# Differential attention with a fp8 feed-forward: the values' lag in branch 2 falls in steps, the first output blocks leave earlier, and TensorE's program ends in one jump

## The chip, the core and the metric

The kernel runs on one core of a Trainium2 chip. The metric is the device time of one execution in microseconds (us), median of several runs. Engines are named as the profile names them: PE is TensorE (PEld its weight loads, PEq its sequencer), DVE is VectorE, ACT is ScalarE, POOL is GpSimd, SP is SyncE, which only issues DMAs here.

## What is computed

The input x has 1024 rows of 256. The output is x plus two terms, both computed from the layer-normalised x. The second term is a gated feed-forward with its operands cast to fp8.

```python
qkv = x @ Wqkv
q1, k1, q2, k2, v = jnp.split(qkv, [C, 2 * C, 3 * C, 4 * C], axis=-1)   # C = 128, 16 heads
A1 = _causal_sdpa(q1, k1, v)
A2 = _causal_sdpa(q2, k2, v)
diff = A1 - lam * A2
rms = jnp.sqrt(jnp.mean(diff * diff, axis=-1, keepdims=True) + EPS)
diff = (1.0 - LAMBDA_INIT) * diff / rms
attn = out @ Wproj            # out: diff with the heads side by side
ffn = _qdot(gelu(_qdot(x, w_gating[0])) * _qdot(x, w_gating[1]), w_linear)
```

`_causal_sdpa` is a causal softmax attention. Each head has queries and keys of 8 and values of 16. So there are two softmaxes (branches 1 and 2) over the same values.

## The kernel before, in words

All matrices of the attention are held transposed: keys on the partitions, queries along the free axis. The 16 heads of a branch are four **groups** of four heads, so both branches make eight groups, g = 0 to 7; groups 4 to 7 are branch 2. The causal score matrix of a head is cut into nine **chunks** of 512 columns (table CHUNKS, c = 0 to 8), some of them in two pieces (kb, wide, q0): the key block, the number of query blocks, the first query. Chunks 0 to 2 finish the queries of the first half (0 to 511); chunk 2 (MIXED) also opens the second half, and chunk 8 (LAST) ends it.

Chunks times four heads are 36 items of a group, taken three at a time: a **unit** n has three score matmuls (`scores`, L898) into one of two PSUM areas, and one exponential of 1536 columns on ACT (L442). A group has 12 units and the whole attention 96 (UNITS). POOL zeroes the upper triangle of the chunks in DIAGONALS (`mask`, L366). Then PE multiplies the exponentials by the values (`values`, L910) into PSUM bank 6, which holds one half of the queries of one group at a time. When a half is done DVE copies it out transposed (`take(g, h)`, L594), and PE may open the next half only after that: `values` of chunk 0 waits on o_taken of the group before, `second_half` on o_taken of the first half.

The order on PE is written out by hand. Unit n issues its scores, then each `values(g, c)` whose `due(g, c)` equals n, then what `beside(n)` finds in tables: the later projections of queries and keys in branch 1, the down-projection of the feed-forward (DOWN_AT) in branch 2. `due` is the unit that ends the chunk plus a **lag** in units (the variable late). PE executes in that order and stops at a wait.

In branch 2 DVE makes, for each half of a group, `difference(i, h)`: divide by the sums, subtract from branch 1's result, square, reduce. `inverse_root` (11 short dependent steps) gives the inverse root mean square of the columns it is called with, `scale_by_root` multiplies by it, and `turn_back(p, h)` transposes two groups' result for the output projection and increments out_t_ready: first (0, 0) and (0, 1) for groups 4 and 5, then (1, 0) and (1, 1) for 6 and 7. PE projects with `project(b, p)` (L941) for each block b of 128 rows and both p; `residual` (L947) adds x plus feed-forward by a product with the identity. POOL has added the feed-forward to x before (`residual`, L372), between its masks. The last half's root comes from ACT (L447). SP and ACT send the rows of out, and SP waits until all five DMAs have landed.

Which of the softmax forms is used (with or without exact row maxima) depends on two flags which PE, DVE and SP load and branch on. With this data both flags are 0 and the plain form runs. PE's program holds the other forms behind it.

Of the kernel before, what the change touches and what calls it, by code (L numbers as in the profile page):

```python
# [6 lines left out]
ALU = mybir.AluOpType  # L7
# [59 lines left out]
Y_BANK = (7, 7, 0, 0, 1, 2, 3, 4)  # L67
# [9 lines left out]
DOWN_AT = {44: (0, 0, 4), 45: (0, 4, 8), 49: (1, 0, 8), 56: (2, 0, 4), 57: (2, 4, 8), 61: (3, 0, 8), 65: (4, 0, 8),  # L77
           68: (5, 0, 4), 69: (5, 4, 8), 73: (6, 0, 8), 79: (7, 0, 4), 80: (7, 4, 8)}
# [41 lines left out]
def diff_attention_ffn_kernel(nc, x, w_qkv, w_proj, lq1, lk1, lq2, lk2, w_gating, w_linear, out):  # L120
# [3 lines left out]
    with ExitStack() as ctx:  # L124
# [117 lines left out]
        def _(sp):  # L242
# [56 lines left out]
            large2 = sp.value_load(flag[0:1, 1:2], min_val=0, max_val=1)  # L299
            with sp.If(large2 == 1):  # L300
# [7 lines left out]
            for n, b in enumerate((0, 2, 4)):  # L308
                sp.wait_ge(y_added, n + 1)
                if b == 4:  # L310
                    sp.wait_ge(y_copied, 1)
                sp.dma_start(out_rows[:, b:b + 2, :], y[:, b:b + 2, :]).then_inc(y_out, 16)
            sp.wait_ge(y_added, 4)
# [4 lines left out]
        def _(pool):  # L318
# [55 lines left out]
            for g in range(GROUPS):  # L374
                for c in sorted(DIAGONALS):
                    mask(g, c)
                    if (g, c) in ((1, 2), (1, 6), (2, 6), (3, 2)):
                        square_of(4 + ((1, 2), (1, 6), (2, 6), (3, 2)).index((g, c)))
                    if (g, c) in ((4, 4), (5, 2), (6, 0), (7, 0)):
                        residual(((4, 4), (5, 2), (6, 0), (7, 0)).index((g, c)))  # L380

        @block.scalar
        def _(act):
# [51 lines left out]
            for n in range(UNITS):  # L435
# [3 lines left out]
                if n * PER_UNIT < KEPT * J and at + PER_UNIT > KEPT * J - 2:  # L439
# [5 lines left out]
                               ).then_inc(exp_done, 1)  # L445
            act.wait_ge(ms_ready, 1)
            act.activation(newton[:, 3, 112:128], newton[:, 0, 112:128], ACT.Sqrt).then_inc(rms_ready, 1)  # L447
            for b in (4, 6):
                act.wait_ge(y_ready, b - 1)
                act.activation(y[:, b, :], ps[:, Y_BANK[b], 0:C], ACT.Copy).then_inc(y_copied, 1)  # L450
            act.wait_ge(y_copied, 2)
            act.dma_start(out_rows[:, 6, :], y[:, 6, :]).then_inc(y_out, 16)

        def bound(dve, own, br):
# [8 lines left out]
            dve.tensor_scalar(flag[0:1, br:br + 1], most[0:1, 5:6], 1.0, None, ALU.add).then_inc(flag_ready, 1)  # L463
# [5 lines left out]
        def _(dve):  # L469
# [136 lines left out]
            def difference(i, h):  # L606

                b, s = slice(16 * h, 16 * h + 16), slice(32 * i + 16 * h, 32 * i + 16 * h + 16)
                take(HG + i, h)
# [78 lines left out]
            keep(3, 1)  # L688

            dve.wait_ge(flag_ready, 2)  # L690
            with dve.If(dve.value_load(flag[0:1, 1:2], min_val=0, max_val=1) == 1):
                maxima(1)

            def add(b):

                dve.wait_ge(res_ready, b // 2 + 1)
                dve.wait_ge(y_ready, b // 2 + 1)
# [29 lines left out]
            add(0)  # L727
            add(2)
            for b in (5, 7):
                dve.wait_ge(y_ready, b - 1)  # L730
                dve.tensor_copy(y[:, b, :], ps[:, Y_BANK[b], 0:C]).then_inc(y_added, 1)

        @block.tensor
        def _(pe):
# [202 lines left out]
            def project(b, p):  # L937

                alone = b >= 4
                at = 0 if alone else b % 2 * C  # L940
                ins = pe.matmul(ps[:, Y_BANK[b], at:at + C], out_t[:, p, b * P:(b + 1) * P], w_p[:, p, :],  # L941
                                start=(p == 0 and at == 0), stop=(p == 1), skip_group_check=True)
                if p == 1 and (alone or b % 2 == 1):
                    ins.then_inc(y_ready, 1)
# [13 lines left out]
            def attention(br, general):  # L958
# [7 lines left out]
                for n in range(n0, n0 + BRANCH):  # L966
# [3 lines left out]
                    if n == UNITS - 2:  # L970
                        pe.wait_ge(wp_in, 16 * 8)
                        pe.wait_ge(ffn_out, TB // 2)
                        pe.wait_ge(out_t_ready, 2)
                        for b in (0, 1):
                            project(b, 0)

            def ending():

                values_due(UNITS, 0, GROUPS)
                for b in (2, 3):  # L980
                    project(b, 0)
                values_due(UNITS + 1, 0, GROUPS)
                pe.wait_ge(out_t_ready, 3)
                for b in range(4):
                    project(b, 1)
                pe.wait_ge(res_ready, TB // 2)
                for b in range(4, TB):
                    project(b, 0)
                    residual(b)
# [49 lines left out]
```

## Time and profile before

| | us |
|---|---|
| median of 3 runs | 199.3 |
| lowest, highest | 198.45, 199.69 |
| the profiled execution, its own time | 199.27 |
| its span, first to last instruction | 197.5 |
| last exponential ends | 180.5 |
| PE's last matmul ends | 189.9 |

The span is 1.77 us shorter than the time of the same execution. The granted clock of PE was 0.993 over the span and 1.00 in every stretch of the attention, that is the level of 2.4 GHz. The span falls into the preparation (0 to 38 us), branch 1 (38 to 110), branch 2 (110 to 180.5) and the end (180.5 to 197.5), in which the last half is finished, projected and sent. A timeline row gives the start, the duration, engine, line, operation, and in brackets how long the engine had been idle before it and who released it. Durations of matmuls overlap their neighbours a little, so starts are the better measure.

### The profile page before, as it was taken

What the parts mean: (1) busy time and instruction counts of PE and PEld (TensorE: products, weight loads), DVE (VectorE), ACT (ScalarE), POOL (GpSimd) and SP (SyncE); (2) the same over time, 40 slices, a digit from 0 to 9 for tenths busy, and PEclk for the clock granted to TensorE, in tenths of its full rate; (3) what the DMA queues carried; (4) which work ended last, traced back from release to release, by engine and by line L of the source; (5) the groups of instructions that cost most, each with busy time, mean ns of one, the idle gap of its engine ahead of it and who ended that gap; (6) DMA issues with size and microseconds to landing.
All of it is one profiled execution on the core that took longest, in us unless ns stands there. A gap on an engine that the chain in (4) does not pass through costs nothing.

```text
span 197.5 us, 3554 instructions
## 1 busy us (share of the span) xinstructions
PE 182.2 (92%) x1446; PEld 78.3 (40%) x1450; DVE 92.4 (47%) x218; ACT 163.6 (83%) x136; POOL 59.4 (30%) x71
## 2 busy tenths in 40 slices
PE   6899989899999999999989999999998999899940
PEld 6855334454332323242333424344342423233830
DVE  0975798431223240540472025216703697895840
ACT  2156865899999999999999999999999899998010
POOL 8526600042216142314442043235216124320000
PEclk9999999999999999999999999999999999999997
DMA  5967377780000000000277781000000000000051
GB/s 174 404 242 245 73 179 205 207 190 10 0 0 3 0 0 3 0 0 3 60 203 188 181 191 39 0 3 0 0 3 0 0 3 0 0 3 0 0 178 44
DMA packets 8149, 14.99 MB, mean 76 GB/s; under 512 B 1984, under 2 KB 5312, under 8 KB 8128
## 3 DMA queue, kind: packets, MB, share of 16 engines
q1 hardware_dynamic: 7440, 14.05, 25.5%
q10 hardware_dynamic: 688, 0.66, 1.0%
q8 instruction: 14, 0.23, 0.5%
q14 instruction: 7, 0.06, 0.1%
HBM read 5.26 MB, written 1.05 MB: 32 GB/s over the span
## 4 chain that ended last, share of the span: by engine, by line
PE 74%; ACT 15%; DVE 4%; POOL 1%; issue 1%; POOLq 0%; DVEq 0%
PE ps L910 29%; PE ps L898 17%; ACT probs L442 13%; PE ps L752 8%; PE ps L758 4%; PE ps L941 4%; PE ps L747 3%; PE ps L851 3%; PE ps L813 3%; DVE area L529 2%; DVE o_t L594 1%; ACT probs L430 1%; PE ps L742 1%; PE ps L947 1%; ACT L430 1%
## 5 line engine op out<-in xcount | busy, mean ns | idle before, releaser
L442 ACT ACTIVATE probs<-ps,shift 128x1536 f32<-128x1536 f32 x96 | 140.1, 1554 | 2.4 <-PE ps L898 1.6
L910 PE MATMUL ps<-probs,v_all 128*32 128x512 f32 (+3 forms) x768 | 78.1, 496 | 1.5 <-DVE o_t L594 1.5
L366 POOL TENSOR_SCALAR_AFFINE_SELECT probs<-probs 128x1024 f32<-128x1024 f32 (+1 forms) x40 | 36.7, 917 | 109.7 <-ACT probs L442 109.6
L898 PE MATMUL ps<-q_st,k_st 32*128 32x512 f32 (+3 forms) x384 | 49.8, 420 | 1.2 <-issue 0.8
L898 PEld LDWEIGHTS ps<-q_st,k_st 32*128 32x128 f32 x384 | 22.4, 182 | 58.6 <-ACT probs L442 30.4
L594 DVE STREAM_TRANSPOSE o_t<-ps 128x512 f32<-128x512 f32 x16 | 11.5, 717 | 49.5 <-PE ps L910 49.5
L910 PEld LDWEIGHTS ps<-probs,v_all 128*32 128x32 f32 x768 | 16.4, 108 | 19.6 <-issue 13.9
L752 PE MATMUL ps<-xn_t,w_q 128*128 128x512 f32 (+1 forms) x38 | 17.3, 557 | 0.8 <-ACT xn_t L393 0.8
L813 PE MATMUL ps<-area 128*128 128x512 fp8e4 x64 | 14.5, 379 | 1.0 <-DVE area L529 1.0
L430 ACT ACTIVATE probs<-ps 128x512 bf16<-128x512 f32 x16 | 9.3, 597 | 4.5 <-PE ps L813 2.7
L529 DVE TENSOR_TENSOR area<-ps,probs 128x512 fp8e4<-128x512 f32 x16 | 10.5, 687 | 1.8 <-ACT probs L430 1.7
L813 PEld LDWEIGHTS ps<-area 128*128 128x128 fp8e4 x64 | 6.0, 97 | 9.5 <-issue 3.4
L758 PE MATMUL ps<-w_q,xn_t 128*128 128x256 f32 x32 | 8.7, 399 | 1.0 <-DVE area L529 1.0
L650 DVE CAST parts<-ps 128x512 fp32r<-128x512 f32 x4 | 2.8, 691 | 14.2 <-PE ps L752 14.1
L752 PEld LDWEIGHTS ps<-xn_t,w_q 128*128 128x128 f32 x38 | 6.2, 189 | 7.3 <-issue 7.0
L851 PE MATMUL ps<-area 128*128 128x256 fp8e4 x64 | 9.1, 275 | 0.0
L941 PE MATMUL ps<-w_p,squares 128*128 128x256 f32 x32 | 8.4, 389 | 0.0
L747 PE MATMUL ps<-ident 128*128 128x128 f32 x36 | 6.8, 378 | 1.6 <-POOL ident L321 1.6
L747 PEld LDWEIGHTS ps<-ident 128*128 128x128 f32 x36 | 6.6, 290 | 1.6 <-POOL ident L321 1.6
L496 DVE TENSOR_TENSOR parts<-ps,parts 128x512 fp32r<-128x512 f32 x8 | 5.5, 690 | 3.5 <-ACT parts L399 3.4
L851 PEld LDWEIGHTS ps<-area 128*128 128x128 fp8e4 x64 | 5.3, 97 | 4.6 <-issue 4.1
L941 PEld LDWEIGHTS ps<-w_p,squares 128*128 128x128 f32 x32 | 5.8, 190 | 2.6 <-issue 1.9
(78 smaller groups left out, 117.2 us busy)
## 6 DMA issues: line engine op xcount, KB each, us to landing
q_st<-parts SPq DMA_DIRECT2D x32, 128.0 KB, 2.8
k_st<-parts SPq DMA_DIRECT2D x32, 128.0 KB, 2.8
probs<-L_ffn_w_gating SPq DMA_DIRECT2D x4, 512.0 KB, 7.8
probs<-L_ffn_w_linear SPq DMA_DIRECT2D x1, 1024.0 KB, 13.1
w_q<-L_attn_Wqkv SPq DMA_DIRECT2D x2, 384.0 KB, 5.8
out<-probs SPq DMA_DIRECT2D x3, 256.0 KB, 3.0
x_sb<-L_attn_x SPq DMA_DIRECT2D x2, 256.0 KB, 4.2
x_sb<-L_attn_x ACTq DMA_DIRECT2D x2, 256.0 KB, 4.5
```

Source lines behind the costliest of these rows:

```text
L366: pool.affine_select(out=blocks, in_=blocks, pattern=pattern, compare_op=ALU.is_ge, fill=0.0, base=0, channel_multiplier=-1).then_inc(mask ...
L442: act.activation(probs[:, at:at + PER_UNIT, :].rearrange("p s u -> p (s u)"), ps[:, 3 * (n % 2):3 * (n % 2) + 3, :].rearrange("p b n -> p ...
L529: dve.tensor_tensor(hidden[:, c, h * HALF:(h + 1) * HALF], ps[:, 2 * PAIR[n] + 1, :], gated[:, n % RING, :], ALU.mult, saturate=False).the ...
L594: dve.transpose(o_t[:, h, :, :].rearrange("p b w -> p (b w)"), ps[:, 6, :]).then_inc(o_taken, 1)
L747: pe.matmul(ps[:, 7, 0:P], ident[:, :], ident[:, :], start=True, stop=True)
L752: return pe.matmul(ps[:, bank, at:at + wide], w_q[:, k, i * P:(i + 1) * P], xn_t[:, k, h * HALF + at:h * HALF + at + wide], start=(k == 0 ...
L758: ins = pe.matmul(ps[:, bank, (b % 2) * C:(b % 2 + 1) * C], xn_t[:, k, b * P:(b + 1) * P], w_q[:, k, 2 * C:3 * C], start=(k == 0), stop=(k ...
L813: ins = pe.matmul(ps[:, 2 * PAIR[n] + g, :], w_gate8[:, g, k, c * P:(c + 1) * P], x8[:, k, h * HALF:(h + 1) * HALF], start=(k == 0), stop= ...
L851: ins = pe.matmul(ps[:, 7, (b % 2) * C:(b % 2 + 1) * C], hidden[:, c, b * P:(b + 1) * P], w_lin8[:, c, :], start=(c == 0), stop=(c == HC - 1))
L898: ins = pe.matmul(ps[:, bank, at:at + wide * P], k_st[rows, g % STACKS, kb * P:(kb + 1) * P], q_st[rows, g % STACKS, queries], start=True, ...
L910: ins = pe.matmul(ps[32 * j:32 * j + 32, 6, q0 % HALF:q0 % HALF + wide * P], v_all[:, g % HG, kb, 32 * j:32 * j + 32], probs[:, slot + j, ...
L941: ins = pe.matmul(ps[:, Y_BANK[b], at:at + C], out_t[:, p, b * P:(b + 1) * P], w_p[:, p, :], start=(p == 0 and at == 0), stop=(p == 1), sk ...
```

## The change

- CHUNKS: chunks 5 and 6 change places, so the second chunk with a diagonal in the second half is now number 5, and DIAGONALS, the squares and one residual on POOL follow.
- The lag of groups 5 and 6 becomes 4 and 3 (before 5 and 4); in group 7 chunks 0 to 5 have 3 and 6 to 8 have 2 (before 0 to 4 have 3, 5 to 8 have 2). DOWN_AT moves some down-projections.
- PE: block 0's and block 1's first projections stand at units 83 and 87 (before both at unit 94), and their second ones ahead of the last two chunks' values; blocks 2 and 3 are projected whole after the values.
- DVE: the takes stand apart from the differences; `inverse_root` is called for 64, 32 and 16 columns (before 64 and 48); blocks 0 and 1 are added before the last take.
- ACT copies blocks 2 and 3 (before DVE added them) and loads the square root's table ahead of that.
- PE's branches are nested so that one jump leads from the end of the used form to the end of the program (before two).

```diff
-    [(1, 4, 512)], [(7, 1, 896), (5, 3, 640)], [(2, 4, 512)], [(3, 4, 512)],
+    [(7, 1, 896), (5, 3, 640)], [(1, 4, 512)], [(2, 4, 512)], [(3, 4, 512)],
...
-DIAGONALS = {0: [0], 1: [0, 128], 2: [0, 256], 4: [0], 6: [0, 128]}
+DIAGONALS = {0: [0], 1: [0, 128], 2: [0, 256], 4: [0], 5: [0, 128]}
...
-Y_BANK = (7, 7, 0, 0, 1, 2, 3, 4)
+Y_BANK = (7, 7, 0, 1, 2, 2, 3, 4)
...
-DOWN_AT = {44: (0, 0, 4), 45: (0, 4, 8), 49: (1, 0, 8), 56: (2, 0, 4), 57: (2, 4, 8), 61: (3, 0, 8), 65: (4, 0, 8),
+DOWN_AT = {44: (0, 0, 4), 45: (0, 4, 8), 49: (1, 0, 8), 53: (2, 0, 8), 56: (3, 0, 4), 57: (3, 4, 8), 61: (4, 0, 8),
...
+Y_AT = {83: 0, 87: 1}
...
-    if g < GROUPS - 2:
-        late = 5
-    elif g < GROUPS - 1:
-        late = 4
-    else:
-        late = (3, 3, 3, 3, 3, 2, 2, 2, 2)[c]
+    late = (5, 5, 5, 5, 5, 4, 3, (3, 3, 3, 3, 3, 3, 2, 2)[min(c, 7)])[g]
...
             all_of, first, last = slice(0, 32), slice(0, 16), slice(16, 32)
-            down(0)
+            take(4, 0)
             own.step(difference(0, 0))
             down(1)
+            take(4, 1)
             own.step(difference(0, 1))
+            take(5, 0)
             own.step(difference(1, 0))
             down(2)
+            take(5, 1)
             own.step(difference(1, 1))
-            own.step(difference(2, 0))
+            take(6, 0)
+            inverse_root(slice(0, 64))
             down(3)
-            inverse_root(slice(0, 64))
             scale_by_root(0, all_of)
             scale_by_root(1, all_of)
             turn_back(0, 0)
             turn_back(0, 1)
+            own.step(difference(2, 0))
+            take(6, 1)
             own.step(difference(2, 1))
+            inverse_root(slice(64, 96))
+            take(7, 0)
+            scale_by_root(2, all_of)
             own.step(difference(3, 0))
-            inverse_root(slice(64, 112))
-            scale_by_root(2, all_of)
+            inverse_root(slice(96, 112))
             scale_by_root(3, first)
             turn_back(1, 0)
+            add(0)
+            take(7, 1)
             difference(3, 1).then_inc(ms_ready, 1)
...
-                    if n == UNITS - 2:
-                        pe.wait_ge(wp_in, 16 * 8)
-                        pe.wait_ge(ffn_out, TB // 2)
-                        pe.wait_ge(out_t_ready, 2)
-                        for b in (0, 1):
-                            project(b, 0)
+                    if n in Y_AT:
+                        if n == min(Y_AT):
+                            pe.wait_ge(wp_in, 16 * 8)
+                            pe.wait_ge(ffn_out, TB // 2)
+                            pe.wait_ge(out_t_ready, 2)
+                        project(Y_AT[n], 0)
             def ending():
+                pe.wait_ge(out_t_ready, 3)
+                project(0, 1)
+                project(1, 1).then_inc(y_ready, 1)
                 values_due(UNITS, 0, GROUPS)
+                values_due(UNITS + 1, 0, GROUPS)
+                pe.wait_ge(res_ready, TB // 2)
                 for b in (2, 3):
                     project(b, 0)
-                values_due(UNITS + 1, 0, GROUPS)
...
-            with pe.If(large1 == 0):
+            with pe.If_eq(mode, 0):
                 attention(0, False)
                 pe.wait_ge(flag_ready, 2)
-                large2 = pe.value_load(flag[0:1, 1:2], min_val=0, max_val=1)
-                with pe.If(large2 == 0):
+                pe.reg_load(mode, flag[0:1, 1:2])
+                with pe.If_eq(mode, 0):
                     second_branch(False)
-                with pe.If(large2 == 1):
-                    second_branch(True)
-            with pe.If(large1 == 1):
...
+            with pe.If_ne(mode, 0):
```

DVE, between the take of group 6's second half and the take of group 7's first half, before. The transpose into o_t is the take, the 128x16 row on newton ends a difference:

```order
L594 STREAM_TRANSPOSE o_t<-ps 128x512
L600 RECIPROCAL r_sum<-o_t 128x16
L601 TENSOR_TENSOR parts<-o_t,r_sum 128x256
L611 SCALAR_TENSOR_TENSOR attn<-parts,neg_lam,attn 128x256
L613 TENSOR_TENSOR parts<-attn 128x256
L614 TENSOR_REDUCE newton<-parts 128x16
L616 TENSOR_SCALAR newton<-newton 128x16
L594 STREAM_TRANSPOSE o_t<-ps 128x512
```

The same place now, from the end of that difference on:

```order
L626 TENSOR_SCALAR halved<-newton 128x32
L627 TENSOR_SCALAR newton<-halved 128x32
L630 SCALAR_TENSOR_TENSOR newton<-newton 128x32
L631 TENSOR_TENSOR newton<-newton 128x32
L632 SCALAR_TENSOR_TENSOR newton<-newton 128x32
L630 SCALAR_TENSOR_TENSOR newton<-newton 128x32
L631 TENSOR_TENSOR newton<-newton 128x32
L632 SCALAR_TENSOR_TENSOR newton<-newton 128x32
L630 SCALAR_TENSOR_TENSOR newton<-newton 128x32
L631 TENSOR_TENSOR newton<-newton 128x32
L632 SCALAR_TENSOR_TENSOR newton<-newton 128x32
L602 STREAM_TRANSPOSE o_t<-ps 128x512
```

The 11 steps of the root of group 6 now stand between the difference and the next take.

PE at the end of its plain form, before (the last three scores, then the ending; L941 is a projection, L947 a residual):

```order
L898 MATMUL ps<-q_st,k_st 128x512 x3
L910 MATMUL ps<-probs,v_all 32x128 x4
L910 MATMUL ps<-probs,v_all 32x384 x4
L910 MATMUL ps<-probs,v_all 32x512 x4
L941 MATMUL ps<-w_p,squares 128x256 x2
L910 MATMUL ps<-probs,v_all 32x512 x4
L941 MATMUL ps<-w_p,squares 128x256 x5
L947 MATMUL ps<-x_sb,ident 128x256
```

And now (L919 scores, L931 values, L961 a projection, L965 a residual):

```order
L919 MATMUL ps<-q_st,k_st 128x512 x3
L931 MATMUL ps<-probs,v_all 32x512 x4
L961 MATMUL ps<-w_p,squares 128x256 x2
L931 MATMUL ps<-probs,v_all 32x512 x8
L961 MATMUL ps<-w_p,squares 128x256
L965 MATMUL ps<-x_sb,ident 128x256
L961 MATMUL ps<-w_p,squares 128x256 x2
L965 MATMUL ps<-x_sb,ident 128x256
L961 MATMUL ps<-w_p,squares 128x256 x5
L965 MATMUL ps<-x_sb,ident 128x256
L961 MATMUL ps<-w_p,squares 128x256 x4
```

One chunk's values stand between the last scores and the two projections, and the last two chunks' values follow them.

## Rows read from the trace of the kernel before

**Rows 1.** The page, part 1: busy us of each engine, share of the span, instructions.

```profile
PE 182.2 (92%) x1446; PEld 78.3 (40%) x1450; DVE 92.4 (47%) x218; ACT 163.6 (83%) x136; POOL 59.4 (30%) x71
```

**Rows 2.** Windows, 158 to 180.5: length, then busy of PE, PEld, DVE, ACT, POOL.

```profile
158.00:180.50 22.50, 21.31 (x205) 7.11 (x202) 19.02 (x47) 21.98 (x17) 6.88 (x7) 1.00 0.01 1
```

**Rows 3.** Timeline of PE in groups 6 and 7: start, duration, line.

```profile
161.00 1.07 PE L910 MATMUL ps<-probs,v_all 128*32 128x512 f32 x8
162.00 0.50 PE L898 MATMUL ps<-q_st,k_st 32*128 32x512 f32 x3
162.71 0.55 PE L898 MATMUL ps<-q_st,k_st 32*128 32x512 f32 x5 [0.21 <-ACT probs L442]
...
168.10 1.07 PE L910 MATMUL ps<-probs,v_all 128*32 128x512 f32 x8 [0.50 <-DVE o_t L594]
...
172.52 0.64 PE L910 MATMUL ps<-probs,v_all 128*32 128x256 f32 x8 [0.48 <-DVE o_t L594]
```

**Rows 4.** Timeline of DVE from the take of (5, 1) to turn_back(0, 1).

```profile
151.23 0.72 DVE L594 STREAM_TRANSPOSE o_t<-ps 128x512 f32<-128x512 f32 x1 [7.62 <-PE ps L910]
...
154.16 0.17 DVE L616 TENSOR_SCALAR newton<-newton 128x16 f32<-128x16 f32 x1
155.74 0.72 DVE L594 STREAM_TRANSPOSE o_t<-ps 128x512 f32<-128x512 f32 x1 [1.41 <-PE ps L910]
...
159.49 0.18 DVE L619 TENSOR_SCALAR halved<-newton 128x64 int32<-128x64 int32 x1
...
163.14 1.42 DVE L630 TENSOR_TENSOR xn_t<-attn,newton 128x512 f32<-128x512 f32 x2
...
164.59 1.30 DVE L634 STREAM_TRANSPOSE squares<-xn_t 128x512 f32<-128x512 f32 x2
```

**Rows 5.** Timeline of DVE from the take of (6, 1) to turn_back(1, 0).

```profile
167.24 0.72 DVE L594 STREAM_TRANSPOSE o_t<-ps 128x512 f32<-128x512 f32 x1 [1.34 <-PE ps L910]
...
168.74 1.20 DVE L611 SCALAR_TENSOR_TENSOR attn<-parts,neg_lam,attn 128x256 f32<-128x256 f32 x1
...
170.88 0.17 DVE L616 TENSOR_SCALAR newton<-newton 128x16 f32<-128x16 f32 x1
...
171.75 0.72 DVE L594 STREAM_TRANSPOSE o_t<-ps 128x512 f32<-128x512 f32 x1 [0.69 <-PE ps L910]
...
175.33 0.19 DVE L619 TENSOR_SCALAR halved<-newton 128x48 int32<-128x48 int32 x1
...
179.92 0.71 DVE L634 STREAM_TRANSPOSE squares<-xn_t 128x512 f32<-128x512 f32 x1
```

**Rows 6.** Timeline of POOL: the masks that fall beside those rows.

```profile
159.86 1.10 POOL L366 TENSOR_SCALAR_AFFINE_SELECT probs<-probs 128x1024 f32<-128x1024 f32 x1 [3.98 <-ACT probs L442]
...
167.31 2.35 POOL L366 TENSOR_SCALAR_AFFINE_SELECT probs<-probs 128x1024 f32<-128x1024 f32 x2
```

**Rows 7.** Timeline of the end: last take, turn_back(1, 1), last projections, last issue.

```profile
182.88 0.72 DVE L594 STREAM_TRANSPOSE o_t<-ps 128x512 f32<-128x512 f32 x1 [2.25 <-PE ps L910]
...
187.02 0.71 DVE L634 STREAM_TRANSPOSE squares<-xn_t 128x512 f32<-128x512 f32 x1
...
188.03 1.89 PE L941 MATMUL ps<-w_p,squares 128*128 128x256 f32 x8
...
191.11 0.50 SPq L314 DMA_DIRECT2D out<-probs  x1
```

**Rows 8.** PE's two last branches by line: duration in ns three times, start us.

```profile
L1008 PEldq COMPARE_BRANCH  x1: 3722/3722/3722, 187.8 to 187.8; - x1
...
L1010 PEldq COMPARE_BRANCH  x1: 5601/5601/5601, 191.6 to 191.6; - x1
```

**Rows 9.** DMA issues from 180 to 198: size each, median us to landing.

```profile
out<-probs SPq DMA_DIRECT2D x3, 256.0 KB, 3.0
out<-probs ACTq DMA_DIRECT2D x1, 128.0 KB, 2.7
out<-probs SPq DMA_DIRECT2D x1, 128.0 KB, 5.1
```

More of the change, by code:

```diff
@@ L298, in _ @@
             sp.wait_ge(flag_ready, 2)
-            large2 = sp.value_load(flag[0:1, 1:2], min_val=0, max_val=1)
-            with sp.If(large2 == 1):
+            large2 = sp.value_load(flag[0:1, 1:2], min_val=0, max_val=2)
+            with sp.If(large2 == 2):
                 sp.wait_ge(max_split[1], 1)
@@ L307, in _ @@
                     maxima(g)
[L308 to L313, printed above, removed]
+            sp.wait_ge(y_added, 1)
+            sp.dma_start(out_rows[:, 0:2, :], y[:, 0:2, :]).then_inc(y_out, 16)
+            sp.wait_ge(y_copied, 2)
+            sp.dma_start(out_rows[:, 2:4, :], y[:, 2:4, :]).then_inc(y_out, 16)
+            sp.wait_ge(y_added, 2)
+            sp.dma_start(out_rows[:, 4:6, :], y[:, 4:6, :]).then_inc(y_out, 16)
+            sp.wait_ge(y_added, 3)
             sp.dma_start(out_rows[:, 7, :], y[:, 7, :]).then_inc(y_out, 16)
@@ L376, in _ @@
                     mask(g, c)
[L377 to L380, printed above, removed]
+                    if (g, c) in ((1, 2), (1, 5), (2, 5), (3, 2)):
+                        square_of(4 + ((1, 2), (1, 5), (2, 5), (3, 2)).index((g, c)))
+                    if (g, c) in ((4, 4), (5, 2), (6, 2), (7, 0)):
+                        residual(((4, 4), (5, 2), (6, 2), (7, 0)).index((g, c)))
         @block.scalar
@@ L445, in _, with whole @@
                                ).then_inc(exp_done, 1)
+            def whole(b):
+                act.wait_ge(y_ready, (1, 2, 4)[(2, 3, 6).index(b)] + 1)
+                act.activation(y[:, b, :], ps[:, Y_BANK[b], 0:C], ACT.Copy).then_inc(y_copied, 1)
+            act.activation(newton[:, 1, 112:113], newton[:, 0, 0:1], ACT.Sqrt)
+            whole(2)
+            whole(3)
             act.wait_ge(ms_ready, 1)
             act.activation(newton[:, 3, 112:128], newton[:, 0, 112:128], ACT.Sqrt).then_inc(rms_ready, 1)
[L448 to L451, printed above, removed]
+            whole(6)
+            act.wait_ge(y_copied, 3)
             act.dma_start(out_rows[:, 6, :], y[:, 6, :]).then_inc(y_out, 16)
@@ L608, in difference @@
                 b, s = slice(16 * h, 16 * h + 16), slice(32 * i + 16 * h, 32 * i + 16 * h + 16)
-                take(HG + i, h)
                 divide(HG + i, h)
@@ L687, in _ @@
             keep(3, 0)
-            keep(3, 1)
             dve.wait_ge(flag_ready, 2)
-            with dve.If(dve.value_load(flag[0:1, 1:2], min_val=0, max_val=1) == 1):
+            large2 = dve.value_load(flag[0:1, 1:2], min_val=0, max_val=2)
+            steps = own.n
+            with dve.If(large2 == 2):
+                keep(3, 1)
                 maxima(1)
+                down(0)
+            own.n = steps
+            with dve.If(large2 == 0):
+                down(0)
+                keep(3, 1)
             def add(b):
                 dve.wait_ge(res_ready, b // 2 + 1)
-                dve.wait_ge(y_ready, b // 2 + 1)
+                dve.wait_ge(y_ready, {0: 0, 4: 3}[b] + 1)
                 dve.tensor_tensor(y[:, b:b + 2, :].rearrange("p b c -> p (b c)"), ps[:, Y_BANK[b], :],
@@ L726, in _ @@
             turn_back(1, 1)
[L727 to L731, printed above, removed]
+            add(4)
+            dve.wait_ge(y_ready, 6)
+            dve.tensor_tensor(y[:, 7, :], ps[:, Y_BANK[7], 0:C], x_sb[:, 7, :], ALU.add).then_inc(y_added, 1)
         @block.tensor
@@ L937, in project @@
             def project(b, p):
[L939 to L944, printed above, removed]
+                at = b % 2 * C if b in (0, 1, 4, 5) else 0
+                return pe.matmul(ps[:, Y_BANK[b], at:at + C], out_t[:, p, b * P:(b + 1) * P], w_p[:, p, :],
+                                 start=(p == 0 and at == 0), stop=(p == 1), skip_group_check=True)
             def residual(b):
```

36 lines of the change are left out of this document (19 added, 17 removed).

## The prediction

> **What bounds the kernel now.** I read the page's busy times first, then windows of branch 2, then PE's timeline unit by unit with the rows of DVE and POOL beside it, and last the end, from the last take to the barrier. PE is busy 182.2 of 197.5 us [rows 1]. In the 22.5 us before the last exponential PE and ACT are both close to full, 21.3 and 22.0 us, and DVE has little left either, 19.0 [rows 2]. So the attention is a relay. A unit costs PE 1.43 us: values take from 161.00 to 162.00, a unit's scores 0.43 after that (starts; the recorded durations overlap a little) [rows 3]. Each wait of PE moves everything behind it, since PE works its order off one after the other. Three kinds stand in these rows: 0.21 us for an exponential (one more like it lies at unit 54), and 0.50 and 0.48 us for a take [rows 3].
>
> Behind the attention comes a fixed tail. The last take starts at 182.88 and the turn_back that it feeds ends at 187.73, 4.85 us later. The four last projections end at 189.92, SP issues the last rows at 191.11 [rows 7], and they have landed 5.1 us later, at 196.2 [rows 9]. But that is not the end of the span: PE's two branches take 3.7 us from 187.8 and 5.6 us from 191.6, so PE is through at 197.19 [rows 8], and the barrier ends 0.35 us behind it. From the end of turn_back (1, 1) to the end of the span it is 9.8 us.
>
> **The end of the program: a gain.** One of the two jumps goes. Its sequencer starts the first as soon as the last projections are queued, 0.1 us behind turn_back (1, 1). With one jump of 3.7 to 5.6 us PE is through 3.8 to 5.7 us after it, and the barrier adds 0.35. The other bound is the output. Blocks 0 to 3 are sent long before now, so the last DMAs find free rings: 0.1 us to the first projection, 1.89 for the four [rows 7], some 0.45 for the last addition (an estimate: 256 columns are half of a transpose-size row of 0.7 [rows 7], and its start adds a little), 0.05 to the issue and 2.7 us to landing, as ACT's DMA of the same size [rows 9], then 0.5 for SP's part of the barrier: 5.7 us. The two bounds nearly meet, and I take 5.8 in place of 9.8: **4.0 us less**. The ends are 3.4 (a landing of 3.0 and a late issue) and 4.2.
>
> The Trainium skill ("Advanced Engine Details and Errata", Control Flow Timing) gives about 108 ns for a compare-and-branch. By that figure the jumps cost 0.2 us together and one less of them would be worth 0.1; the sum would then have only the output's part. The trace disagrees with it at this place by a factor of over thirty [rows 8]. "Runtime: NRT & Kernel Launch" (Instruction fetch mechanics) has the exception that fits: a taken branch to a page that isn't loaded waits for a fetch by DMA.
>
> **The lag and the order: new waits of PE.** PE's work is the same: two projections (1 us) leave the stretch ahead of the last take and two others enter it. Values earlier means scores later in PE's queue, so the last exponential ends later and less is left behind it. What counts is the last take, which is PE's work plus its waits. I go through these.
>
> Unit 65: values(4, 8) and values(5, 0) come in neighbouring units now, with only scores between, as at units 77 and 88 before. That is a wait for a take like the one of 0.50 [rows 3]. **+0.5.**
>
> Unit 83: the first projection waits for turn_back (0, 1), which ended at 165.89 before, unnoticed. The take of (6, 0) ends at 156.5 as before. Then come the root of 64 columns, 3.65 us (159.49 to 163.14), down(3), 0.65 us (159.49 less 155.74 less a difference of 3.10, which is 151.23 to 154.33), and scaling and turning back, 2.75 us (163.14 to 165.89) [rows 4]: 163.55. PE has finished values(6, 5) at 162.0, and scores of one unit stand behind that: 162.4 [rows 3]. **+1.3** with the semaphore; 0.9 to 1.5. Before this wait everything behind it queues, the scores of unit 84 and so ACT first.
>
> Unit 91: second_half(7) waits for the take of (7, 0), and this take now stands behind the root of 32 columns. A difference took 3.10 us with nothing beside it [rows 4] and 3.81 at 167.24, because the scalar_tensor_tensor at 168.74 took 1.20 and ended 0.28 us after the second of two masks that ran to 169.66 [rows 5, 6]. Now the take of (6, 1) comes a little earlier against POOL's residual and masks, so I put two blocked operations, 4.2. The root's steps of 64 columns took 3.65 with a mask beside them [rows 4, 6], so 2.9 without one (the block costs 3.81 less 3.10), and 32 columns I take at 2.7. With the take of 0.72 and a semaphore: 7.8 us after the take of (6, 1) started. PE got to second_half 4.80 us after that start (172.52 less its wait of 0.48) [rows 3, 5]. Now one projection and one unit's scores replace its wait of 0.50 at unit 88, 5.2 us. **+2.6.** If no operation is blocked it is 1.4, and if a third is, 3.5.
>
> The ending: the first second-half projection waits for turn_back (1, 0), and the last two chunks' values stand behind it. DVE needs from the take of (7, 0) 3.1 to 3.6 us to its root (171.75 to 175.33) [rows 5], 2.6 for 11 steps, 1.2 for two scalings and 0.7 to turn back: 7.6 to 8.1. PE reaches the wait after 7.15: 0.86 for the take, 0.57 for second_half, four times scores and values of 1.43. **+0.7**; 0.5 to 1.0.
>
> Gone are 0.4 of waits for exponentials, 0.50 at unit 88 and 0.48 at unit 91 [rows 3]: **-1.4.** Added up: 0.5 + 1.3 + 2.6 + 0.7 - 1.4 = **3.7 us later** for the last take, between 1.9 and 5.1. The chain behind the last take stays 4.85 us. Block 0's addition stands ahead of that take and is covered, since the take waits for two chunks' values. ACT's table load and its two copies lie behind the last exponential beside PE's work; if that cover went they would be 0.4 us each. Masks in other places, POOL's residual and SP's earlier DMAs gain or cost nothing where PE doesn't wait for them. DVE's extra branch falls into its idle time before unit 52.
>
> **The sum.** Last take 182.9 + 3.7 = 186.6, turn_back 191.4, span 191.4 + 5.8 = 197.2, and with the 1.77 us around the span 199.0 against 199.27 of the same execution. That execution lies at the median of 199.3. I predict **199.1**.
>
> **Rivals.**
>
> *DVE is not blocked (faster), 0.20.* If its operations miss POOL's masks, the waits are 0.5 + 0.9 + 1.4 + 0.5 less 1.4 = 1.9, and the time 197.2 or somewhat under. For it: all seven steps of the difference at 151.23 ran free [rows 4]. Against: there are masks beside both chains in this trace, and each cost 0.7. The Trainium skill ("SBUF — State Buffer", the reading of its diagram) speaks against it too: DVE and GpSimd share a port pair as an exclusive lock, and an operation of DVE with two inputs in SBUF waits for the whole instruction of GpSimd. Row 168.74 agrees [rows 5].
>
> *The jump's fetch holds the last rows (slower), 0.14.* The last DMA took 5.1 us to land where ACT's took 2.7 [rows 9], while PE fetched for its second jump [rows 8]. If the single jump's fetch falls on the last DMAs, the same 2.4 us come back: 201.4. The point from which it decides is a fetch later than 2.7 us behind turn_back (1, 1), when these DMAs start; the first jump was through 3.8 us behind it, so its fetch was earlier than that.
>
> *The one jump costs as much as both, 0.03.* PE through at 191.5 + 9.3 = 200.8, time 202.9.
>
> **Chances.** My forecast, gain and loss of equal size, has 0.63. A measurement of this kernel tells about 1%, 2 us, from no change. Within that: 0.63; faster 0.20; slower 0.17. The range takes in the unblocked case and the held rows: 196.8 to 201.5.
>
> **What would show it.** Right: PE idle at unit 91 for 2 us and more with the take named, and at unit 83 for about 1; last exponential ending between 183 and 184; last take at 186 to 187; one compare-and-branch at PE's end; from turn_back (1, 1) to the end 5.5 to 6 us. Wrong: a take of (7, 0) at its old distance from that of (6, 1), 4.5 us, or a last landing more than 4 us behind its issue.

## The result: slower by 0.9%, 201.05 us where 199.1 was predicted

| | before | changed kernel |
|---|---|---|
| median of 8 runs, us | 199.19 | 201.05 |
| lowest, highest | 198.45, 199.69 | 199.99, 203.52 |
| the profiled execution, its own time | 199.27 | 200.71 |
| its span | 197.5 | 198.6 |
| last exponential ends | 180.5 | 185.9 |
| last take starts | 182.88 | 188.32 |

The ratio is 1.009 (95% interval 1.0074 to 1.0107). The time lies inside the predicted range (196.8 to 201.5) and less than 1% above the kernel before, but the kernel is slower, by 1.9 us, where I had gain and loss of equal size. (One run, 203.52, lies over 1.5% above the fastest and does not count in the ratio.)

The page of the changed kernel, part 1, answers to [rows 1]: PE is busy 2.9 us longer with two instructions more, and DVE's ten more are the 11 steps of the third root, with one addition less.

```profile
PE 185.1 (93%) x1448; PEld 78.2 (39%) x1448; DVE 95.3 (48%) x228; ACT 165.6 (83%) x138; POOL 59.3 (30%) x71
```

PE's waits by line, 108 to 190 (total, times, longest). The take is now waited for 3.8 us in all, once for 2.8, and a turn_back 1.3:

```profile
PE ps L931 <- DVE o_t L602: 3.8, 3, 2.8
PE ps L961 <- DVE squares L641: 1.3, 1, 1.3
```

PE's timeline in the changed kernel, which answers to [rows 3] (start, duration, line; L961 a projection, L931 values, L919 scores). The first row is unit 83, the row with 2.83 us is second_half at unit 91:

```profile
164.09 0.67 PE L961 MATMUL ps<-w_p,squares 128*128 128x256 f32 x2 [1.31 <-DVE squares L641]
...
174.09 0.55 PE L919 MATMUL ps<-q_st,k_st 32*128 32x128 f32 x6
177.47 0.64 PE L931 MATMUL ps<-probs,v_all 128*32 128x256 f32 x8 [2.83 <-DVE o_t L602]
178.03 0.59 PE L919 MATMUL ps<-q_st,k_st 32*128 32x512 f32 x3
178.56 1.94 PE L931 MATMUL ps<-probs,v_all 128*32 128x512 f32 x8
180.43 0.80 PE L919 MATMUL ps<-q_st,k_st 32*128 32x512 f32 x3
181.15 1.32 PE L931 MATMUL ps<-probs,v_all 128*32 128x512 f32 x8
182.40 0.50 PE L919 MATMUL ps<-q_st,k_st 32*128 32x512 f32 x3
...
185.26 1.13 PE L961 MATMUL ps<-w_p,squares 128*128 128x256 f32 x4
```

The last row, the pair of projections in the ending, has no wait before it. Both waits lie where the prediction put them, at 1.3 and 2.8 us (1.3 and 2.6 predicted). What it had not is what follows the second: the same eight values that take 1.07 us in [rows 3] take 1.94, and the next scores and values are long too. Windows of the same kernel (length, busy of PE, PEld, DVE, ACT, POOL, then granted clock) show why:

```profile
158.00:172.00 14.00, 12.69 (x108) 4.11 (x107) 10.31 (x22) 13.11 (x10) 4.69 (x5) 1.00 0.00 1
172.00:178.00 6.00, 3.17 (x45) 1.29 (x42) 5.49 (x17) 4.89 (x4) 2.05 (x3) 1.00 0.00 0
178.00:183.00 5.00, 5.00 (x37) 1.24 (x37) 4.45 (x17) 3.13 (x3) 0.06 (x1) 0.66 0.01 3
```

PE had stood idle for 2.83 us; after it the granted clock was 0.66 over 5 us, a mix of the levels 2.4 and 1.2 GHz. PE counts as fully busy there, so part 1's share rose while less was done. In starts, the three groups took 1.87, 0.72 and 1.25 us where 1.00, 0.43 and 1.00 are usual: 1.4 us lost.

DVE over the same stretch, which answers to [rows 5]: take of (6, 1), two long operations, the first step of the root of 32 columns, the take of (7, 0), and turn_back(1, 0).

```profile
169.28 0.72 DVE L602 STREAM_TRANSPOSE o_t<-ps 128x512 f32<-128x512 f32 x1 [3.10 <-PE ps L931]
...
170.32 1.10 DVE L609 TENSOR_TENSOR parts<-o_t,r_sum 128x256 f32<-128x256 f32 x1
171.46 1.20 DVE L618 SCALAR_TENSOR_TENSOR attn<-parts,neg_lam,attn 128x256 f32<-128x256 f32 x1
...
173.81 0.18 DVE L626 TENSOR_SCALAR halved<-newton 128x32 int32<-128x32 int32 x1
...
175.60 0.61 DVE L630 SCALAR_TENSOR_TENSOR newton<-newton 128x32 f32<-128x32 f32 x1
...
176.69 0.72 DVE L602 STREAM_TRANSPOSE o_t<-ps 128x512 f32<-128x512 f32 x1
...
183.79 0.71 DVE L641 STREAM_TRANSPOSE squares<-xn_t 128x512 f32<-128x512 f32 x1
```

POOL beside it, which answers to [rows 6]:

```profile
170.04 2.34 POOL L364 TENSOR_SCALAR_AFFINE_SELECT probs<-probs 128x1024 f32<-128x1024 f32 x2
175.53 0.63 POOL L364 TENSOR_SCALAR_AFFINE_SELECT probs<-probs 128x512 f32<-128x512 f32 x1 [3.15 <-ACT probs L440]
```

DVE's two long operations end behind the first and the second mask, and a root's step is stretched from 0.19 to 0.61 us while the third mask runs. The take at 176.69 has no idle time in brackets: from 169.28 on DVE was busy all the way to it. The takes of (6, 1) and (7, 0) lie 7.41 us apart, before it was 4.51 [rows 5].

The end: turn_back(1, 1), PE's branch, the last issue, and the landings, against [rows 7 to 9].

```profile
192.45 0.71 DVE L641 STREAM_TRANSPOSE squares<-xn_t 128x512 f32<-128x512 f32 x1
```

```profile
L1031 PEldq COMPARE_BRANCH  x1: 3485/3485/3485, 193.2 to 193.2; - x1
```

```profile
195.71 0.36 SPq L312 DMA_DIRECT2D out<-probs  x1
```

```profile
out<-probs SPq DMA_DIRECT2D x3, 256.0 KB, 2.2
out<-probs ACTq DMA_DIRECT2D x1, 128.0 KB, 2.5
out<-probs SPq DMA_DIRECT2D x1, 128.0 KB, 2.5
```

One branch of 3.5 us is left, PE is through at 196.7, and the last rows land 2.5 us after their issue, at 198.2. SP ends the span. From the end of turn_back(1, 1), 193.16, it is 5.4 us to the end, 4.4 less than before (4.0 predicted). So in this pair of executions the last take came 5.4 us later and 4.4 went out behind the last turn_back: +1.1 in the span.

### The profile page after: what moved, and what is told of

Its sections match the earlier page's. It is cut to its first block, busy times and chain, and to the rows that moved or that the text cites. A ratio compares the mean times of both kernels' runs of the same rounds, so it can differ in the third digit from the quotient of the medians.

```text
span 198.6 us, 3563 instructions
## 1 busy us (share of the span) xinstructions
PE 185.1 (93%) x1448; PEld 78.2 (39%) x1448; DVE 95.3 (48%) x228; ACT 165.6 (83%) x138; POOL 59.3 (30%) x71
## 4 chain that ended last, share of the span: by engine, by line
PE 77%; DVE 12%; ACT 7%; issue 1%; POOL 1%; POOLq 0%; DVEq 0%
PE ps L931 31%; PE ps L919 17%; PE ps L773 8%; ACT probs L440 4%; PE ps L779 4%; PE ps L961 4%; PE ps L872 4%; PE ps L768 4%; PE ps L834 3%; DVE area L537 2%; DVE o_t L602 2%; DVE newton L630 1%; DVE newton L632 1%; ACT probs L428 1%; PE ps L763 1%
## 5 line engine op out<-in xcount | busy, mean ns | idle before, releaser
L440 ACT ACTIVATE probs<-ps,shift 128x1536 f32<-128x1536 f32 x96 | 141.6, 1539 | 6.0 <-PE ps L919 5.3
L931 PE MATMUL ps<-probs,v_all 128*32 128x512 f32 (+3 forms) x768 | 79.4, 502 | 3.8 <-DVE o_t L602 3.8
L919 PE MATMUL ps<-q_st,k_st 32*128 32x512 f32 (+3 forms) x384 | 50.3, 423 | 0.0
L919 PEld LDWEIGHTS ps<-q_st,k_st 32*128 32x128 f32 x384 | 22.6, 183 | 59.6 <-issue 29.9
L931 PEld LDWEIGHTS ps<-probs,v_all 128*32 128x32 f32 x768 | 16.3, 109 | 22.1 <-issue 14.2
L961 PE MATMUL ps<-w_p,squares 128*128 128x256 f32 x32 | 8.5, 394 | 1.3 <-DVE squares L641 1.3
L961 PEld LDWEIGHTS ps<-w_p,squares 128*128 128x128 f32 x32 | 5.7, 189 | 4.4 <-issue 2.4
```

Of the source, the lines that this page charges most:

```text
L440: act.activation(probs[:, at:at + PER_UNIT, :].rearrange("p s u -> p (s u)"), ps[:, 3 * (n % 2):3 * (n % 2) + 3, :].rearrange("p b n -> p ...
L919: ins = pe.matmul(ps[:, bank, at:at + wide * P], k_st[rows, g % STACKS, kb * P:(kb + 1) * P], q_st[rows, g % STACKS, queries], start=True, ...
L931: ins = pe.matmul(ps[32 * j:32 * j + 32, 6, q0 % HALF:q0 % HALF + wide * P], v_all[:, g % HG, kb, 32 * j:32 * j + 32], probs[:, slot + j, ...
L961: return pe.matmul(ps[:, Y_BANK[b], at:at + C], out_t[:, p, b * P:(b + 1) * P], w_p[:, p, :], start=(p == 0 and at == 0), stop=(p == 1), s ...
```

## The experiments

Each was timed in 5 rounds beside the kernel before; ratios are to it, with the 95% interval. On the loss I held two theories: (1) the take of (7, 0), behind the root of 32 columns, stops PE, and the stop also costs clock; (2) the values' earlier order itself costs, through the scores that come later. On the gain: what the jump is worth by itself, and what the earlier output.

**One jump alone, in the kernel before.** DVE now writes 2 in place of 1 into the second flag when it is set, so that the nested branches can tell the cases apart; with this data it stays 0.

```diff
-            large1 = pe.value_load(flag[0:1, 0:1], min_val=0, max_val=1)
-            with pe.If(large1 == 0):
+            mode = pe.alloc_register("mode")
+            pe.reg_load(mode, flag[0:1, 0:1])
+            with pe.If_eq(mode, 0):
...
-            with pe.If(large1 == 1):
...
+            with pe.If_ne(mode, 0):
...
```

> The kernel before with only PE's branches nested so that one jump ends its program. Theory A (the second jump, 5.6 us from 191.6 to 197.2, set the end of the span, and its fetches held the last rows' landing at 5.1 us): PE is through at about 191.5, the last DMA lands 2.7 us behind its issue at 191.1, span about 194.3, time 196.0 (3.3 us less than before). Theory B (the landing of 1 MB of output takes until 196.2 anyway): span 196.7, time 198.5.

197.39 us, ratio 0.991 (0.989 to 0.9931): 1.8 less, between the two expectations (196.0 and 198.5). Its branch and its landings:

```profile
L1009 PEldq COMPARE_BRANCH  x1: 3785/3785/3785, 187.8 to 187.8; - x1
```

```profile
out<-probs SPq DMA_DIRECT2D x3, 256.0 KB, 3.1
...
out<-probs SPq DMA_DIRECT2D x1, 128.0 KB, 4.4
```

The second jump took 5.6 us [rows 8], yet removing it gave only 1.8, since the last DMA still needs 4.4 us (5.1 before) behind the other output. From the end of turn_back(1, 1), 187.73, it is 8.2 us to the end of the span, 1.6 less than before.

**The changed kernel with two jumps.** PE's branches as before; nothing else.

```diff
-            with pe.If_ne(mode, 0):
...
+                with pe.If(large2 == 2):
+                    second_branch(True)
+            with pe.If(large1 == 1):
```

> The changed kernel with PE's branches as before, so two jumps. Theory A: the first jump ends at 196.7 as now, the second takes 3.5 to 5.6 us more, span 200.6 to 202.7 in place of 198.6, time 203 to 205 (2 to 4 us over the changed kernel). Theory B (of the 4.4 us that the end got shorter the earlier output is all): no change, 201.

204.49 us, ratio 1.0287 (1.0251 to 1.0323): 3.4 more than the changed kernel. The two jumps took 3.6 and 5.1 us:

```profile
L1031 PEldq COMPARE_BRANCH  x1: 3622/3622/3622, 195.5 to 195.5; - x1
```

```profile
L1033 PEldq COMPARE_BRANCH  x1: 5137/5137/5137, 199.2 to 199.2; - x1
```

With the output out early, the jump decides. Its price is best read behind turn_back(1, 1), where the clock of the attention has no part: from the end of turn_back(1, 1), 195.39, it is 9.2 us to the end of the span, against 5.4 with one jump. So the stretch is 9.8 us before, 8.2 with one jump alone, 9.2 with the earlier output alone and 5.4 with both. Of the 4.4 us gained neither part gives much alone, 1.6 and 0.6; they need each other.

This trace shows something else. Up to the ending the order is that of the changed kernel, and so are the two waits, but this was the slowest of the six executions (206.77 us), and the clock fell behind the wait of 1.31 us at unit 83 too:

```profile
163.72 1.04 PE L961 MATMUL ps<-w_p,squares 128*128 128x256 f32 x2 [1.31 <-DVE squares L641]
...
165.42 1.94 PE L931 MATMUL ps<-probs,v_all 128*32 128x512 f32 x8
```

```profile
164.00:168.00 4.00, 4.00 (x22) 1.00 (x25) 1.67 (x5) 1.65 (x3) 0.00 (x0) 0.59 0.00 0
178.00:183.00 5.00, 4.36 (x26) 1.01 (x27) 4.66 (x12) 1.61 (x2) 1.10 (x1) 0.50 0.02 3
```

From the projection at unit 83 to the second values behind it PE took 4.06 us where it took 2.51 in the changed kernel's trace, and behind unit 91 it lost 1.1 us more than there. Counted from the first exponential of branch 2 the last take comes 2.6 us later than in the changed kernel's trace. So the same order pays a different price for the clock from one execution to the next, and a wait of 1.3 us can be enough.

**The take ahead of the root.** The take of (7, 0) goes right behind the difference of (6, 1), one root of 48 columns behind the difference of (7, 0), as before the change.

```diff
             own.step(difference(2, 1))
-            inverse_root(slice(64, 96))
             take(7, 0)
-            scale_by_root(2, all_of)
             own.step(difference(3, 0))
-            inverse_root(slice(96, 112))
+            inverse_root(slice(64, 112))
+            scale_by_root(2, all_of)
```

> The changed kernel with the take of (7, 0) right behind the difference of (6, 1), and one root of 48 columns behind the difference of (7, 0), as before. Theory A (the loss is PE's wait at unit 91 and the clock that falls behind it): the wait goes from 2.8 to about 0.4, the clock stays at its upper level, values(7, 3) take 1.0 us again, the wait for turn_back (1, 0) becomes 1.4; last take 3.4 us earlier, time 197.6. Theory C (the steps of the lag cost, wherever the take stands): under 1 us, time 200 to 201.

197.23 us, ratio 0.9918 (0.9897 to 0.994): 3.8 less than the changed kernel. PE at unit 91, then the windows:

```profile
175.05 0.64 PE L930 MATMUL ps<-probs,v_all 128*32 128x256 f32 x8 [0.39 <-DVE o_t L602]
...
176.05 1.06 PE L930 MATMUL ps<-probs,v_all 128*32 128x512 f32 x8
```

```profile
172.00:178.00 6.00, 5.61 (x67) 1.98 (x64) 5.21 (x11) 6.00 (x5) 2.10 (x3) 1.00 0.01 3
178.00:183.00 5.00, 3.68 (x39) 1.19 (x32) 4.19 (x15) 4.98 (x5) 0.07 (x1) 1.00 0.00 0
```

The wait is 0.39 in place of 2.83, the clock stays at 1.00, and the last take comes at 185.78, 2.5 earlier (3.4 expected). That is 2.4 of wait plus 1.4 of clock, less 1.3: PE now reaches the ending early enough to wait that long for turn_back(1, 0). Both executions begin branch 2 at the same time, 110.45 and 110.44. The medians lie 3.8 apart, more than the 2.5 of this pair; a likely reason is that the clock costs more in other executions of the changed kernel, as in the trace above. Two of this kernel's twelve executions took 199.0 and 198.8 us at a granted clock of 0.991, where the others have 0.997 and more: a fall behind one of the waits of 1.3 us that are left would do that, but they have no trace. Nothing of the lag was touched, so the net loss of 1.9 us needs no theory (2). That the steps of the lag cost nothing is not shown by this: the last take is still 2.9 us later than before.

**The stop kept, the clock held.** Before PE's wait at unit 91 stand 34 products of a zero tile with ones, added into a bank whose values they don't change. They do no useful work; the wait, the take and DVE's order stay.

```diff
+                if g == GROUPS - 1:
+                    pe.wait_ge(ones_set, 1)
+                    for _ in range(FILL):
+                        pe.matmul(ps[:, 7, 0:P], zeros[:, :], ones[:, :], start=False, stop=False,
...
```

> The changed kernel with 34 products of a zero tile, 128 columns each, added into bank 7 ahead of PE's wait at unit 91, so that PE is busy for some 2 us of the 2.8. Theory A2 (the wait costs twice: by itself, and by the clock, which fell to about half behind it): the wait stays as long counted from unit 91's scores, but values(7, 3) to (7, 4) run at the upper level, last take 1.3 to 1.5 us earlier, time 199.5. Theory D (PE's slow stretch from 177.5 to 182.4 has another cause than the idle PE): no change, 201, or slower if the products outlast the wait.

199.54 us, ratio 1.0029 (1.0011 to 1.0047): 1.5 less than the changed kernel, by adding work. PE, and the window that read 0.66:

```profile
174.00 2.07 PE L960 MATMUL ps<-ones,zeros 128*128 128x128 bf16 x34
176.89 0.64 PE L934 MATMUL ps<-probs,v_all 128*32 128x256 f32 x8 [0.82 <-DVE o_t L605]
...
177.89 1.07 PE L934 MATMUL ps<-probs,v_all 128*32 128x512 f32 x8
...
183.98 1.13 PE L969 MATMUL ps<-w_p,squares 128*128 128x256 f32 x4 [0.74 <-DVE squares L644]
```

```profile
178.00:183.00 5.00, 5.00 (x49) 1.30 (x47) 4.38 (x19) 4.99 (x4) 0.00 (x0) 1.00 0.00 0
```

PE starts second_half when the take allows it, as before, and the clock does not fall behind it. And the ending's wait of 0.74, which the prediction had at 0.7, is there: in the changed kernel the slow stretch had covered it. So in this pair of executions the clock's net price is 1.4 less 0.74, about 0.7 (from the first exponential of branch 2 to the last take it is 77.14 us here and 77.88 there). The medians say 1.5. Over the span the granted clock was 0.996 or more in 11 of this kernel's 12 runs (the twelfth: 0.991 and 201.25 us). In the changed kernel it was 0.99 in the profiled run and two others, 199.99 to 200.71 us, but 0.983 in four, 200.85 to 201.5. Those four have no trace; the trace with two jumps shows two ways in which the clock can cost more, a longer fall behind unit 91 and one behind unit 83.

**The first projections later.** Units 87 and 91 in place of 83 and 87.

```diff
-Y_AT = {83: 0, 87: 1}
+Y_AT = {87: 0, 91: 1}
```

> The changed kernel with block 0's and 1's first projections at units 87 and 91 in place of 83 and 87, nothing else. Theory A (the waits of PE add up, the one at unit 83 with 1.3 us): this wait is gone, the one at unit 91 stays between 2.3 and 2.8 with the clock's fall behind it, last take 1.1 to 1.3 us earlier, time 199.9. Rival (what is gained at unit 83 is lost again at unit 91, since the take of (7, 0) is DVE's chain and not PE's): the wait at unit 91 grows by as much, time 201.

199.64 us, ratio 1.0053 (1.0023 to 1.0083): 1.4 less than the changed kernel. The wait of 1.3 for turn_back(0, 1) is gone (waits 108 to 190):

```profile
PE ps L931 <- DVE o_t L602: 3.6, 3, 2.6
PE ps L919 <- ACT probs L440: 0.6, 2, 0.3
```

The stop at unit 91 is still 2.6, and the clock falls behind it as before (0.92 over 172 to 178, 0.75 over 178 to 183). So what is gained at unit 83 is not lost again at unit 91. Counted from the first exponential of branch 2 the last take comes only 0.7 us earlier in the traces (two new waits of 0.3 for an exponential take part of it), and the medians' 1.4 holds a part of the clock that differs between executions: four of these twelve took 201.0 to 202.7 us at 0.974 to 0.983.

**Both edits.** The last two together.

```diff
-Y_AT = {83: 0, 87: 1}
+Y_AT = {87: 0, 91: 1}
...
-            inverse_root(slice(64, 96))
             take(7, 0)
```

> The take of (7, 0) ahead of one root of 48 columns, and the projections at units 87 and 91. Theory A: of the waits at units 83 and 91 at most 0.4 us is left, the one for turn_back (1, 0) is about 1.0; last take near 184.3, end 5.3 us behind turn_back (1, 1), time 195.9. Rival (the two mend the same loss): no better than the first alone, 197.2.

196.16 us, ratio 0.9856 (0.9832 to 0.9879): faster than before by 1.4%, where the change as it stood was slower. Left at the ending is a wait of 1.0 for turn_back(1, 0).

**The pair of second projections behind the values.** That wait has the last two chunks' values behind it; now they go first, and the addition of blocks 0 and 1 goes behind the last difference.

```diff
             def ending():
+                values_due(UNITS, 0, GROUPS)
+                values_due(UNITS + 1, 0, GROUPS)
                 pe.wait_ge(out_t_ready, 3)
                 project(0, 1)
                 project(1, 1).then_inc(y_ready, 1)
-                values_due(UNITS, 0, GROUPS)
-                values_due(UNITS + 1, 0, GROUPS)
```

> As the one before, and the pair of projections of blocks 0 and 1 that waits for turn_back (1, 0) stands behind the last two chunks' values, block 0's and 1's addition behind the last difference. Theory A: the wait and the 1.06 us of the pair leave the stretch ahead of the last take (2.0 us), but PE's work behind it grows to 5.9 us and becomes longer than DVE's chain of 4.9, which gives 1 back: time 195.0. Rival (the output's early start is worth more than the order of the values): 196.5.

195.13 us, ratio 0.9801 (0.9778 to 0.9824), 1.0 less than with both edits alone (195.0 expected).

**The old lag, with the pair ahead of the values.** The kernel of both edits with the lag of groups 5 and 6, and the down-projections, as before the change.

```diff
-    late = (5, 5, 5, 5, 5, 4, 3, (3, 3, 3, 3, 3, 3, 2, 2)[min(c, 7)])[g]
+    late = (5, 5, 5, 5, 5, 5, 4, (3, 3, 3, 3, 3, 3, 2, 2)[min(c, 7)])[g]
```

> As the second, but the lag of groups 5 and 6 and the table of down-projections as in the kernel before (5 and 4). Theory A (PE is the bound and the lag only orders its work, so the steps of the lag bring nothing): within 0.5 us of the second, 195.9. Rival C (the steps cost, by the wait for a take at unit 65 and the scores that come later): 1 us less, 194.9. Rival E (the steps gain, since less is left at the end): 1 us more, 196.9.

195.87 us, ratio 0.9843 (0.9819 to 0.9867), beside 0.9856 with the steps: no difference that counts.

**The loss put into the kernel before.** The root of 32 columns ahead of the take of (7, 0), which `difference(3, 0)` then no longer makes itself; nothing else of the change.

```diff
-            own.step(difference(3, 0))
-            inverse_root(slice(64, 112))
+            inverse_root(slice(64, 96))
+            take(HG + 3, 0)
             scale_by_root(2, all_of)
+            own.step(difference(3, 0))
+            inverse_root(slice(96, 112))
```

> The kernel before with one thing of the change alone: DVE's root of 32 columns (group 6) stands ahead of the take of (7, 0), and a root of 16 behind the difference. Lag, projections, jumps as before. Theory A (this place makes the loss, with the lag of before too): PE waits 2.5 to 2.8 us at unit 91 in place of 0.48, the clock falls behind it, last take 3.4 to 3.7 us later, time 202.7. Theory A without the clock's fall: 201.4. Rival (it costs only together with the steps of the lag): under 1 us, 199.5.

202.67 us, ratio 1.016 (1.0122 to 1.0198): 3.4 slower. PE at the place, and the windows:

```profile
174.32 0.64 PE L913 MATMUL ps<-probs,v_all 128*32 128x256 f32 x8 [2.63 <-DVE o_t L594]
```

```profile
172.00:178.00 6.00, 3.68 (x30) 1.31 (x34) 5.45 (x18) 3.68 (x4) 0.63 (x1) 0.83 0.01 3
178.00:183.00 5.00, 5.00 (x42) 1.96 (x38) 3.23 (x10) 3.33 (x3) 1.10 (x1) 0.86 0.00 0
```

The old lag, the old chunks, the old ending, and the same stop and fall of the clock. This one placement costs 3.4 us by itself. One of its six executions had a granted clock of 0.994, as high as in any execution of the kernel before, and took 201.18 us, 1.9 more than before; without the clock's fall 201.4 was expected. The others read 0.970 to 0.980 and took 202.2 us and more.

**The fastest version.** Both edits, the pair behind the values, and the old lag.

> The fastest so far (take of (7, 0) first, projections at units 87 and 91, the pair behind the last values) with the lag and the down-projections of the kernel before. With the pair moved, what is left at the end stands in front of the last take in both. Theory A (the steps of the lag neither gain nor cost, PE's work is the same): within 0.4 us of 195.1. Rival: the steps gain once the waits are gone, 196 and more.

193.97 us, ratio 0.9737 (0.9722 to 0.9752), 7.1 less than the changed kernel. The expectation, within 0.4 of 195.1, missed: it is 1.2 less than the same with the steps. ACT's last exponentials, first here and then in the kernel with the steps, show it:

```profile
175.58 4.40 ACT L440 ACTIVATE probs<-ps,shift 128x1536 f32<-128x1536 f32 x3
180.00 1.28 ACT L451 ACT_TABLE_LOAD   x1
```

```profile
175.13 5.91 ACT L440 ACTIVATE probs<-ps,shift 128x1536 f32<-128x1536 f32 x4
181.06 1.28 ACT L451 ACT_TABLE_LOAD   x1
```

And their last takes, in the same order:

```profile
181.17 0.72 DVE L602 STREAM_TRANSPOSE o_t<-ps 128x512 f32<-128x512 f32 x1 [0.58 <-PE ps L930]
```

```profile
182.23 0.72 DVE L602 STREAM_TRANSPOSE o_t<-ps 128x512 f32<-128x512 f32 x1 [1.15 <-PE ps L930]
```

With the pair moved away nothing stands between the last exponential and the last values. It ends 1.1 us earlier with the old lag, and the take comes 1.1 us earlier (0.15 of it lies ahead of branch 2). With the pair ahead of the values the last values had to wait for turn_back(1, 0), which comes only 0.3 us earlier with the old lag (a wait of 1.3 us in place of 1.0), and that hid most of it. So the steps do cost about 1 us through later scores, as theory (2) has it, but only once nothing else holds the last values.

## Why the prediction was wrong, step by step

- **What bounds it.** Right in the main: taking out PE's waits moved the last take earlier each time. Once the pair stood behind the values, the last exponential set it (the fastest version).
- **One jump, 4.0 less.** Right: 4.4. The last landing took 2.5 (2.7 taken), the branch 3.5. The prediction had the two bounds nearly equal. PE was through 3.5 us behind turn_back(1, 1) and the last rows had landed 5.0 behind it, so the output sets the end now; the gain needed both parts (1.6 and 0.6 alone). The figure of 108 ns in "Advanced Engine Details and Errata" (Control Flow Timing) of the Trainium skill would have made the jump worth 0.1: the runs contradict it at this place.
- **Unit 65, +0.5**, and **unit 83, +1.3.** Right for the waits: the waits for a take besides unit 91's are two of 0.5 (3.8 less 2.8), the one at unit 65 new, the other at unit 77 there before. Unit 83 read 1.31; its removal gave 0.7 in the traces and 1.4 in the medians. The clock can fall behind this wait too, which cost 1.5 us in the trace with two jumps, and the term had no room for that.
- **Unit 91, +2.6.** The wait was right, 2.8, with two blocked operations of DVE and one step more; the two operations ended 0.28 us behind the end of a mask. That agrees with the rule of the Trainium skill ("SBUF — State Buffer", SBUF: two separate sides) of a port pair that DVE and GpSimd lock each other out of. **This is the step that failed: the term was priced as the wait alone.** PE's clock fell behind it, and the same values and scores took 1.4 us more; with the clock held the median was 1.5 less. The kernel before had no PE wait near 2.8 us in the attention, and its clock read 1.00 in every stretch; I carried that reading over to an order in which PE stands idle over four times as long as it did at any place there (0.65 at most, and 0.50 in branch 2 [rows 3]). "TensorE: Matmul & The Clock Gate" (What's actually happening) of the Trainium skill says that the gate follows how busy the array has been, with the throttled level as default. The trace agrees: 1.00 before the stop, 0.66 behind it. I had read it and made no term of it.
- **The ending, +0.7.** Not there, since the slow stretch made PE later than turn_back(1, 0). It is there, 0.74, in the run with the clock held.
- **Gone, -1.4.** Right in kind: no wait for an exponential is left in that stretch.
- **The sum, +3.7 for the last take.** It was +5.4: 3.7 with 1.4 of clock, 0.2 of wait more at unit 91, 0.37 by which this execution began branch 2 later (110.44, before 110.07), and less 0.7 at the ending, is 4.97. Some 0.5 us are not placed.
- **Rivals.** "DVE is not blocked" fell: two operations were. "The jump's fetch holds the last rows" fell: 2.5 us to landing. "The one jump costs as much as both" fell: 3.5 us. The case that came was none of them: it was the forecast's own chain with a price for the clock added.
- **Chances.** The forecast's point was off by 2 us. With the clock's term, 1.4 less the ending's 0.7, the sum would have been 199.8, and the side slower. With the clock held the median was 199.54, near the forecast. The rest up to the 201.05 measured fits executions in which the clock cost more, up to 2.6 us more in the trace with two jumps; no trace of the changed kernel's own slower executions shows it.

## What to carry to other kernels

A copy out of PSUM for which the matmul engine waits belongs ahead of any long chain of short dependent steps on the copying engine: one such chain of 2.9 us moved here from behind a take to ahead of it cost 3.4 us by itself. Where an edit gives a nearly full PE a wait of 2.6 us or more, price the wait and then the slow clock behind it, here about half as much again in one trace and more in others; in one execution a wait of 1.3 us was enough. A reading of 1.00 in the old trace says nothing about the new order. A second jump at the program's end was worth 1.8 us where late output hid most of it and 3.4 where the output left early: look at what ends next before a term is priced. A large change should be taken apart before it is dropped: of this one the single jump and the earlier output, together, are worth keeping. With the take and the first projections moved it is 1.4% faster than before, with the pair of projections behind the values 2.0%, and with the old lag too 2.6%.

## What the runs showed of the hardware that was not expected

- Behind an idle stretch of PE of 2.6 to 2.8 us the granted clock was 0.66 over the next 5 us here (0.92 and 0.75 over 172 to 178 and 178 to 183 with the projections later, 0.83 and 0.86 in the kernel before with the root first). Behind a wait of 1.3 us it stayed at 1.00 in four traces (the changed kernel, the take ahead of the root, the clock held, the old lag), and fell to 0.59 over the next 4 us in one (two jumps). Behind waits of 1.0 us and less it stayed at 1.00 in all traces. Small matmuls of 2.07 us laid into the stretch kept it at 1.00.
- A taken branch at the end of PE's program lasted 3.4 to 3.9 us, and a second right behind it 5.1 to 5.6. The last output DMA took 5.1 and 5.2 us to land behind 768 KB with two jumps (the kernel before, and the one with the root first), 4.4 behind the same with one, and 2.4 to 2.5 where most of the output had gone before. Whether the 0.7 between two jumps and one comes from the second jump or is chance of one execution stays open.
